# Weighted values of an attention kernel with the probabilities as the stationary operand

## The reference, cut to what matters

```python
x = x + jnp.tanh(g_xattn[0]) * cross(layernorm(x), ctx)   # fp8 block-quantised x @ ctx.T, 4 x 512 x 512
h = layernorm(x)
fused = h @ (Wa * col_scale)                    # 512 -> 1536: queries, keys, values
q, k, v = ...                                   # 16 heads of 32
scores = jnp.einsum('bhtd,bhsd->bhts', Qf, Kf) * scale
scores = jnp.where(causal, scores, finfo.min)
attn = jax.nn.softmax(scores, axis=-1)
out = jnp.einsum('bhts,bhsd->bhtd', attn, V)    # the weighted values
y = out.transpose(0, 2, 1, 3).reshape(B, T, C)
return x + jnp.tanh(g_ffn[0]) * (y @ Wp)
```

## Time and profile before

| | us |
|---|---|
| median of 3 runs | 531.11 (529.98 to 533.79) |
| the profiled execution | 531.24 |
| its span, first to last instruction | 529.5 |
| mean granted TensorE clock over the span | 0.959 |

### The profile page before, as it was taken

The page is one execution under the profiler, slowest core; times in us unless marked ns, Lnnn a source line. Parts: engine busy times, 40 slices in busy tenths (PEclk is TensorE's granted clock), DMA queues, the critical chain, the costliest instruction groups (busy, mean ns, idle before and its releaser), DMA issues.

```text
span 529.5 us, 7878 instructions
## 1 busy us (share of the span) xinstructions
PE 458.1 (87%) x2536; PEld 325.8 (62%) x2536; DVE 336.6 (64%) x1110; ACT 272.3 (51%) x530; POOL 144.5 (27%) x264
## 2 busy tenths in 40 slices
PE   0477777998889999998779999998898999999994
PEld 0355556765555788765554878865564878676762
DVE  4997442698995244598996242677997244556634
ACT  2994326695545461595636452495655324444430
POOL 5849161252215200243214300233122100111210
PEclk9999997999878999999987999998989999999999
DMA  6411434323500245314400244314400143333002
GB/s 232 165 34 48 158 85 105 81 49 96 145 2 2 71 105 159 95 35 101 138 19 2 51 104 136 125 26 99 98 6 2 45 102 93 82 95 106 22 20 80
DMA packets 28025, 42.62 MB, mean 80 GB/s; under 512 B 8272, under 2 KB 8528, under 8 KB 27984
## 3 DMA queue, kind: packets, MB, share of 16 engines
q1 hardware_dynamic: 26448, 41.97, 28.5%
q10 hardware_dynamic: 1536, 0.14, 0.2%
HBM read 12.59 MB, written 4.19 MB: 32 GB/s over the span
## 4 chain that ended last, share of the span: by engine, by line
PE 58%; ACT 18%; DVE 13%; SPq 3%; issue 3%; DMA 2%; POOL 2%; ACTq 1%; DVEq 0%; POOLq 0%
PE pv_bank L716 11%; PE mm_bank L564 7%; PE mm_bank L565 6%; PE mm_bank L566 6%; PE exp_bank L702 5%; DVE x_all L1201 5%; PE max_bank L685 5%; ACT work L984 4%; DVE max_bank L1235 3%; SPq L374 3%; PE mm_bank L743 2%; PE mm_bank L744 2%; PE mm_bank L745 2%; PE turn_bank L580 2%; ACT tile_buf L931 2%
## 5 line engine op out<-in xcount | busy, mean ns | idle before, releaser
L1235 DVE CUSTOM_DVE_ANT_0 max_bank<-max_bank,causal 128x512 f32<-128x512 f32 (+3 forms) x256 | 119.2, 517 | 65.4 <-PE max_bank L685 65.0
L482 POOL TENSOR_SCALAR_AFFINE_SELECT work<-work 128x384 f32<-128x384 f32 x64 | 33.4, 521 | 299.4 <-ACT work L984 299.4
L984 ACT ACTIVATE work<-exp_bank 128x512 f32<-128x512 f32 (+1 forms) x192 | 90.9, 526 | 25.5 <-PE exp_bank L702 24.5
L716 PE MATMUL pv_bank<-work,v_aug 128*33 128x256 f32 (+3 forms) x512 | 83.6, 473 | 0.0
L702 PE MATMUL exp_bank<-q_stack,k_stack 97*128 97x512 f32 (+3 forms) x256 | 68.9, 353 | 4.1 <-ACT work L984 1.6
L685 PE MATMUL max_bank<-k_stack,q_stack 96*128 96x512 f32 (+3 forms) x256 | 61.7, 342 | 10.4 <-DVE row_max L1235 6.5
L716 PEld LDWEIGHTS pv_bank<-work,v_aug 128*33 128x33 f32 x512 | 29.0, 118 | 54.2 <-issue 48.5
L1218 DVE SCALAR_TENSOR_TENSOR qk_lo<-mm_bank,col_root,qk_hi 128x512 fp32r<-128x512 f32 x32 | 24.0, 750 | 59.2 <-ACT qk_hi L957 59.1
L1201 DVE SCALAR_TENSOR_TENSOR x_all<-mm_bank,coef,x_all 128x128 f32<-128x128 f32 x224 | 61.0, 342 | 0.8 <-PE mm_bank L612 0.8
L685 PEld LDWEIGHTS max_bank<-k_stack,q_stack 96*128 96x128 f32 x256 | 45.9, 196 | 17.8 <-issue 7.0
L702 PEld LDWEIGHTS exp_bank<-q_stack,k_stack 97*128 97x128 f32 x256 | 43.3, 188 | 19.7 <-ACT work L984 9.0
(11 more groups left out here) (161 smaller groups left out, 812.6 us busy)
## 6 DMA issues: line engine op xcount, KB each, us to landing
q_stack<-qk_hi SPq DMA_DIRECT2D x128, 64.0 KB, 2.0
k_stack<-qk_hi SPq DMA_DIRECT2D x128, 64.0 KB, 2.0
x_all<-in_x SPq DMA_DIRECT2D x16, 256.0 KB, 4.0
ctx_raw<-in_ctx SPq DMA_DIRECT2D x16, 256.0 KB, 4.4
q_stack<-qk_lo SPq DMA_DIRECT2D x64, 64.0 KB, 2.0
k_stack<-qk_lo SPq DMA_DIRECT2D x64, 64.0 KB, 2.0
out<-x_all SPq DMA_DIRECT2D x16, 256.0 KB, 2.3
work<-in_L_ffn_Wa SPq DMA_DIRECT2D x3, 768.0 KB, 9.7
```

Of the source, the lines that this page charges most:

```text
L482: pool.affine_select(out=three, in_=three, compare_op=ALU.is_ge, fill=0.0, base=0, pattern=[[0, 3], [1, P]], channel_multiplier=-1)
L716: last = pe.matmul(pv_bank[64 * j:64 * j + D + 1, P * m:T], v_aug[:, m, 2 * u + j, :], prob[j][:, PROB_COL[m]:PROB_COL[m] + T - P * m], st ...
L984: act.activation(prob[j][:, UNIT_COL[k]:UNIT_COL[k] + UNIT_LEN[k]], exp_bank[(3 * j + k) % 2][:, 0:UNIT_LEN[k]], ACT.Exp, scale=SCALE).the ...
L1235: last = dve.tensor_tensor_reduce(max_bank[unit % 2][:, col:col + width], max_bank[unit % 2][:, col:col + width], causal[:, T - width:T], ...
```

## The change

The two operands of the weighted values change places. For each head j, each block of queries i and each block of keys m up to i, the block of probabilities (128 x 128) is stationary and the 33 columns of `v_aug` move; sums over m build up in 33 columns of the bank, at (i, j). The rows of the result are the queries, so nothing is left to be turned: `copy_values`, `turn_values`, the tile `values`, the clearing of the bank and the semaphores s_cleared, s_pvcopy and s_pvt go, and with them the T entries of TensorE's and ScalarE's lists. VectorE's normalising waits for s_pv and reads the bank in another order of (i, j). ScalarE gets two waits on s_pv, ahead of the first exponential of a step and of the copy of the next batch's values, which the removed copy had implied.

```diff
-PV_ROWS = 64 + D + 1
...
-PE_END = "k1 P0 M0 V0 T0 V1 M1 y0 y1 y2 M2 V2 y3 O0 O1 O2 O3"
+PE_END = "k1 P0 M0 V0 V1 M1 y0 y1 y2 M2 V2 y3 O0 O1 O2 O3"
-ACT_END = "k1 T0 c1 V0 c2 y0 V1 y1 y2 V2 c3 y3"
+ACT_END = "k1 c1 V0 c2 y0 V1 y1 y2 V2 c3 y3"
...
-    "PE": "P0 Z4 Z5 Z6 Z7 T0 z3 Z8 Z9 Z10 Z11",
-    "ACT": "T0 z3",
+    "PE": "P0 Z4 Z5 Z6 Z7 z3 Z8 Z9 Z10 Z11",
+    "ACT": "z3",
...
-        values = sb("values", [P, T])
...
         pv_bank = pb("pv_bank")
+        pv_rows = pv_bank[:, 0:NT * 2 * (D + 1)].rearrange("p (i j e) -> p i j e", i=NT, j=2)
...
                 pe.wait_ge(s_causal, 8 * b + u + 1)
-                for m in range(NT):
-                    for j in range(2):
-                        last = pe.matmul(pv_bank[64 * j:64 * j + D + 1, P * m:T], v_aug[:, m, 2 * u + j, :],
-                                         prob[j][:, PROB_COL[m]:PROB_COL[m] + T - P * m],
-                                         start=(m == 0), stop=(m == NT - 1))
+                for j in range(2):
+                    for i in range(NT):
+                        for m in range(i + 1):
+                            col = PROB_COL[m] + P * (i - m)
+                            last = pe.matmul(pv_rows[:, i, j, :], prob[j][:, col:col + P], v_aug[:, m, 2 * u + j, :],
+                                             start=(m == 0), stop=(m == i))
                 last.then_inc(s_pv, 1)
-
-            def turn_values(b, u):
-
-                pe.wait_ge(s_pvcopy, 8 * b + u + 1)
-                for i in range(NT):
-                    last = pe.transpose(pv_bank[:, P * i:P * i + PV_ROWS], values[0:PV_ROWS, P * i:P * i + P],
-                                        ident[0:PV_ROWS, 0:PV_ROWS])
-                last.then_inc(s_pvt, 1)
...
-                    if u:
-                        turn_values(b, u - 1)
...
                     act.wait_ge(s_v, NT * n + i + 1)
+                    if n:
+                        act.wait_ge(s_pv, 8 * n)
...
-            def copy_values(b, u):
-                act.wait_ge(s_pv, 8 * b + u + 1)
-                act.activation(values[0:PV_ROWS, :], pv_bank[0:PV_ROWS, :], ACT.Copy).then_inc(s_pvcopy, 1)
-
             def exponentials(b, u, j, k):
+                if j == k == 0:
+                    act.wait_ge(s_pv, 8 * b + u)
                 act.wait_ge(s_st, 48 * b + 6 * u + 3 * j + k + 1)
...
-                dve.wait_ge(s_pvt, 8 * b + u + 1)
-                pv = pv_bank[:].rearrange("p (i j e) -> p j i e", j=2, i=NT)
+                dve.wait_ge(s_pv, 8 * b + u + 1)
+                pv = pv_rows.rearrange("p i j e -> p j i e")
...
-            dve.memset(pv_bank[:], 0.0).then_inc(s_cleared, 1)
```

More of the change, by code:

```diff
@@ L269, in flamingo_block @@
         s_const, s_sign = sem("s_const"), sem("s_sign")
-        s_cleared = sem("s_cleared")
         s_gates, s_small = sem("s_gates"), sem("s_small")
@@ L307, in flamingo_block @@
         s_pv = sem("s_pv")
-        s_pvcopy, s_pvt = sem("s_pvcopy"), sem("s_pvt")
         s_norm = sem("s_norm")
@@ L772, in late_half @@
                 out_product(B - 2, half // 2, (2, 3) if half % 2 else (0, 1))
-            pe.wait_ge(s_cleared, 1)
             pe.wait_ge(s_const, 1)
@@ L883, in body @@
                         weighted_values(b, STEPS - 1)
-                    elif kind == "T":
-                        turn_values(b, STEPS - 1)
                     elif kind == "M":
@@ L1099, in body @@
                     fill(gaps[u][1])
-                    if u:
-                        copy_values(b, u - 1)
                     fill(gaps[u][2])
@@ L1109, in body @@
                 for kind, i in pieces(ACT_END if more else END_LAST["ACT"], more, ctx_more):
-                    if kind == "T":
-                        copy_values(b, STEPS - 1)
-                    elif kind == "y":
+                    if kind == "y":
                         y_hi(i)
```

## The result

The changed kernel takes 679.71 us (median of 4 runs, 668.62 to 683.13) against 530.55 before (527.91 to 533.79), and the ratio is 1.268 (95% interval 1.250 to 1.286). Times are medians of all runs; a ratio and its interval are of the runs in the faster of a kernel's two states alone, where the changed kernel took 668.62 and 677.23 us, and its profiled execution, of 682.19 us, is not one of them. The kernel is slower by 149 us, which is the direction that was forecast, 27 us above the predicted 653 and inside the range of 555 to 715. Its time varies more from run to run than before.

What follows compares the result with a forecast made beforehand. TensorE, busy 87% of the span, was taken to bound the kernel. 531 + 68 (weighted values) - 12 (turns) - 13 (waits) - 1 (end) = 573 us, + 80 for the falling clock = 653 us, range 555 to 715.

Steps and rivals of the forecast that it cites:

- Load-bound pairs, 0.11 us: Weighted values on TensorE: the load sets the pace, each load-and-matmul pair starting 0.11 us after the last at full clock.
- the 4.4 of the sum: Weighted values, per step: 40 pairs at 0.11 us make 4.4 us in place of 2.28, bounds 2.2 and 7.8.
- Loads slow with the clock: Weighted values on TensorE: loads slow at the lower clock, starting 0.2 us apart, the product taking about 8 us.
- The clock falls because little is streamed: Weighted values: the array streams about a quarter of the time, so the clock falls in nearly each step.
- the first rival: Whole kernel: the clock holds and loads set the pace, 573 us (555 to 590), chance 0.28.
- The clock's term: Weighted values at the lower clock: 8 us in 28 of 32 steps, 224 us less 47 already there, costing +80 us.
- The sum at full clock: Whole kernel at an unchanged clock: 531 + 68 - 12 - 13 - 1 = 573 us.
- +68: Weighted values on TensorE: (4.4 - 2.28) x 32 us added, with nothing covering it.
- The turns' 14 us: TensorE's turns of the values, removed: 0.45 x 32 = 14 us, counted as -12 because some is waited for elsewhere.
- The waits' -13: TensorE's four longest waits for VectorE and ScalarE, 19.5 us: two thirds vanish as those engines catch up, -13 us.
- Turns and end, -13: Removed turns in each step, -12 us, and the wait before the last block's turn at the end, -1 us.
- The cheap-load rival: Weighted values: loads as cheap as fp8 ones, 0.056 us a pair, 2.24 us a step, 517 us in all, chance 0.06.

Runs made afterwards that it cites:

- wide128: The changed kernel with 128 moving columns instead of 33 in the weighted values, groups reordered so surplus is overwritten: 581.77 us.
- split: The changed kernel with the weighted values of the two heads in two places of the step, head 1 where the turns were: 650.13 us.
- wide64: The changed kernel with 64 moving columns instead of 33 in the weighted values, same loads: 614.48 us.
- wide48: The changed kernel with 48 moving columns instead of 33 in the weighted values: 660.44 us.
- noturn: The kernel before without ScalarE's copy of the values and TensorE's turns: 525.96 us against 530.84, ratio 0.995.

## Why the prediction came out as it did

- **Load-bound pairs, 0.11 us: right.** 40 pairs of the product take 4.38 us at full clock, as against the 4.4 of the sum. That they overlap with the matmul before is right as well. The widths add the proof: 33 or 128 columns, the same 4.38.
- **Loads slow with the clock: right.** 8.39 us for the product at the lower level, 0.21 us a pair, as read from the earlier trace rows in advance.
- **The clock falls because little is streamed: right, and shown** by the widths alone: with 33, 48, 64 and 128 columns under the same loads, the profiled executions have 310, 252, 147 and 21 us at the lower level and take 682.2, 661.3, 628.1 and 577.9 us. That the clock holds and 573 comes out was the first rival; it is what wide128 is, not what the change does.
- **The clock's term: mis-sized, in two factors that partly cancel.** I took 224 us at the lower level, in 28 stretches of 8; 310 were measured. Most of the stretches are as short as I took them, but three are not (columns as in the earlier trace rows):

```profile
152.00:210.00 58.00, 55.70 (x225) 50.43 (x225) 27.87 (x100) 16.48 (x33) 12.17 (x26) 0.50 0.08 24
330.00:367.00 37.00, 35.96 (x146) 33.23 (x146) 15.10 (x54) 11.90 (x24) 9.35 (x18) 0.50 0.00 1
490.00:527.00 37.00, 35.98 (x146) 33.42 (x146) 12.58 (x44) 10.12 (x21) 4.45 (x12) 0.50 0.00 1
```

  They are 132 us at 0.50 and hold the seven products that take 8.39 us; the clock did not come back between one product and the next. And I took 0.455 us lost for each us at the lower level. Between profiled executions it is less: from wide128 to the changed kernel 104 us for 289, 0.36; to split 69 for 201, 0.34; to wide64 50 for 126, 0.40; to wide48 83 for 231, 0.36. TensorE's idle time shrank from 44.0 us (516 - 472.00) to 27.6 (620 - 592.45), which is 16 of the 40 us by which 104 falls short of half of 289; where the rest lies is open. Forecast +80, measured +98 by the medians. With the 263 us that the profiles have more than before, at my 0.455, the term would have been +120 and the forecast 693: that it came within 27 us is in part luck.
- **The sum at full clock: 573, measured 581.8.** The profiled executions of wide128 and of the kernel before are 46.6 us apart, and TensorE is busy 45.4 us more (472.00 against 426.60) and idle 1.1 more. The product is the first part: from each product's start to the next instruction's, the 32 of them last 142.8 us in wide128 and 82.5 before, which is +60 and not +68, since I counted 2.28 us for every product before, and several had met the lower level (the one in the earlier trace rows, for example). The turns' 14 us are the rest. The waits' -13 is wrong: the four longest are 20.2 us where they were 19.5, and only at the lower clock did 8 of them go.
- **Turns and end, -13: too large by noturn**, which gives 3 to 5 us and at most 6. The two profiles of the point before have room for the whole 14. The evidence does not agree to better than some 10 us, so how much of the 0.45 us a step is only waited for elsewhere stays open; the sum took it for 2 of 14.
- **The cheap-load rival** was rightly given little for fp32. With bf16 loads it comes true as to the product (0.5 us), and still does not come true as to the time, because the 57 us taken from the product came back, with a DMA wait of 33.4 us and a lower clock. I had not named this cover in the prediction: a product of 2.28 us hid that DMA nearly fully.
- The Trainium skill's advice in "TensorEngine Tiling (Array Packing)", section "When to Use Tiling", to swap and tile by columns when the moving side is 64 columns or fewer, agrees with the result: undoing it costs 4.38 in place of 2.28 us a product, 1.9 times, near the page's "up to 2x". The runs bear it out for fp32 alone; with bf16 operands the two orders are level. The question left open by "TensorE: Matmul & The Clock Gate", section "What's actually happening", whether loads count as busy, is answered for this kernel: loads busy 4.00 of 4 us (168 to 172) left the clock at 0.50.

What stays open: why the time varies by some 2% between runs of the changed kernel. The clock over the span differs between its runs too (0.754 to 0.777), but nothing here steers where a fall begins. And how much of noturn's 3 to 5 us is the copy and how much the turns was not tried apart.

## What to carry to other kernels

Count a product by its loads as well as by its columns: here an fp32 load of 128 stationary columns cost 0.11 us at full clock and 0.21 at the lower, twice per matmul, with 33 to 128 columns streamed. A stretch that loads much and streams little looked busy in this profile (4.00 of 4 us) and still brought the clock down, so price it at both levels and read the granted clock behind it. Before shortening work on the busiest engine, ask which transfer it covers and whether its columns are what holds the clock.

## What the runs showed of the hardware that I had not expected

- Adding columns that nobody reads made a kernel faster by 98 us (679.7 to 581.8), since the loads covered them (4.38 us a product in both) and the clock held (0.98 against 0.75).
- 20 pairs of bf16 loads of 128 columns with 33 moving span 0.67 us; less the 0.18 us that the last one lasts it is 0.026 us each, a quarter of the fp32 pair, and half of the fp8 pair in the earlier trace rows, which streams 128 columns.
- Cutting a product from 2.28 to about 0.5 us a step in the kernel that TensorE bounds at 87% changed the time by less than 1% (533.9 against 530.8), in either order of operands.
